# Merging the two halves' token lists of the first sequence before the second sequence's search

## What is computed

```python
r = sigmoid(x @ Wr.T); k = x @ Wk.T; v = x @ Wv.T
scaled = k * v / clip(scale, 1e-10)         # scale = exp(pos * log(sigmoid(decay)))
out = r * cumsum(scaled, axis=1) * scale
normed = (out - mean) * rsqrt(var + eps)    # mean and var over the whole sequence
x = x + (normed * gn_weight + gn_bias) @ Wo.T
```

```python
top_vals, top_idx = top_k(xf @ w_router.T, 4)
g = silu(x_ec @ w_gate[e]); u = x_ec @ w_up[e]
contrib = ((g * u) @ w_down[e]) * w_ec      # added to the tokens' rows
combined = combined + (silu(xf @ w_sh_gate) * (xf @ w_sh_up)) @ w_sh_down
```

## Time and profile before

| | us |
|---|---|
| median of 3 runs | 709.51 |
| lowest and highest | 709.04, 709.54 |
| the profiled execution | 709.04 |
| its span in the trace | 707.2 |
| PE busy | 666.2 (94%) |
| DVE busy | 325.5 (46%) |
| ACT busy | 161.2 (23%) |
| POOL busy | 219.7 (31%) |

### The profile page before, as it was taken

How to read it: one execution, slowest core, us unless ns; L and a number is a source line. 1 busy time by engine, 2 the same in 40 slices (tenths; PEclk the granted TensorE clock), 3 DMA queues, 4 the chain that set the end, 5 groups by cost and what they waited for, 6 DMA issues and landing times. The chain is left out here.

```text
span 707.2 us, 8987 instructions
## 1 busy us (share of the span) xinstructions
PE 666.2 (94%) x3227; PEld 401.1 (57%) x3227; DVE 325.5 (46%) x784; ACT 161.2 (23%) x259; POOL 219.7 (31%) x209
## 2 busy tenths in 40 slices
PE   3999999999999999999999999999999999999881
PEld 2587878878878754455445454554554554544330
DVE  5887567859958771322323323323232333232220
ACT  4833114623211411111112112111111211111110
POOL 4637546535548131021221121212212022212111
PEclk9999999999999999999999999999999999999996
DMA  8201015722775987599999999999999999999972
GB/s 323 71 1 60 1 31 186 263 73 98 289 294 197 355 309 270 212 359 370 405 396 394 371 387 387 404 382 376 388 403 396 359 395 397 391 401 371 388 272 40
DMA packets 52347, 202.67 MB, mean 287 GB/s; under 512 B 7331, under 2 KB 7459, under 8 KB 51920
## 3 DMA queue, kind: packets, MB, share of 16 engines
q1 hardware_dynamic: 36512, 169.23, 60.6%
q0 software_dynamic: 8928, 21.33, 12.7%
q10 hardware_dynamic: 6864, 11.54, 4.4%
HBM read 178.66 MB, written 23.59 MB: 286 GB/s over the span
## 5 line engine op out<-in xcount | busy, mean ns | idle before, releaser
L617 POOL DMA_INDIRECT out_dram<-ym,midx x32 | 51.3, 1603 | 302.8 <-DVE ym L1224 129.4
L1560 PE MATMUL bank<-w_sb,xT 128*64 128x384 f32 x768 | 129.4, 489 | 1.3 <-ACT xT L840 0.8
L1348 PE MATMUL bank<-x_hi,w_parts 128*128 128x512 f32 x368 | 114.9, 395 | 5.0 <-DVE x_lo L953 3.4
L1581 PE MATMUL bank<-w_sb,guT 128*64 128x512 f32 x384 | 88.0, 593 | 3.2 <-issue 2.4
L1560 PEld LDWEIGHTS bank<-w_sb,xT 128*64 128x64 f32 x768 | 52.9, 137 | 64.7 <-issue 59.7
L1348 PEld LDWEIGHTS bank<-x_hi,w_parts 128*128 128x128 f32 x368 | 69.4, 189 | 21.3 <-DVE x_lo L953 4.2
L1348 PE MATMUL bank<-x_lo,w_parts 128*128 128x512 f32 x184 | 71.0, 395 | 0.0
L1164 DVE TENSOR_TENSOR gu<-sg,bank 128x384 f32<-128x384 f32 x32 | 17.7, 554 | 111.4 <-issue 104.5
L1481 PE MATMUL bank<-sh_sb,xS 128*128 128x384 f32 x192 | 63.9, 486 | 0.0
L1581 PEld LDWEIGHTS bank<-w_sb,guT 128*64 128x64 f32 x384 | 27.7, 137 | 52.1 <-issue 51.4
L1481 PEld LDWEIGHTS bank<-sh_sb,xS 128*128 128x128 f32 x192 | 35.7, 191 | 22.3
(11 more groups left out here) (181 smaller groups left out, 949.3 us busy)
## 6 DMA issues: line engine op xcount, KB each, us to landing
w_sb<-in_L_ffn_w_down SPq DMA_DIRECT2D x64, 768.0 KB
w_sb<-in_L_ffn_w_gate SPq DMA_DIRECT2D x48, 768.0 KB
w_sb<-in_L_ffn_w_up SPq DMA_DIRECT2D x48, 768.0 KB
extra<-in_L_ffn_w_gate SPq DMA_DIRECT2D x16, 768.0 KB
extra<-in_L_ffn_w_up SPq DMA_DIRECT2D x16, 768.0 KB
ring<-in_L_attn_x SPq DMA_DIRECT2D x14, 256.0 KB, 3.4
xt_dram<-xwT ACTq DMA_DIRECT2D x12, 256.0 KB, 3.2
xS<-xt_dram SPq DMA_DIRECT2D x12, 256.0 KB, 14.3
```

Source lines behind the costliest of these rows:

```text
L617: pool.indirect_dma_start(out=out[:, :], out_offset=bass.IndirectOffsetOnAxis(ap=midx[j % 3][u][:, :], axis=0), in_=ym[u][:, :], in_offset ...
L1348: ins = pe.matmul(ps[u][:, :], w, xp, start=(n == 0), stop=(n == len(parts) - 1))
L1560: ins = pe.matmul(ps[e * C:(e + 1) * C, 0:I], xT[:, c, e * C:(e + 1) * C], gate_up(2 * j + u, e, k)[:, c, :], start=(c == 0), stop=(c == K ...
L1581: ins = pe.matmul(pair_bank(j, u)[e * C:(e + 1) * C, :], guT[0][:, c, e * C:(e + 1) * C], down(2 * j + u, e)[:, c, :], start=(c == 0), sto ...
```

## The change

In the first search the results go to `best` instead of `key`, and the last round raises `best_ready`. PE gets one more product, `move_best(0)`, between its steps S+5 and S+6: it waits for that semaphore and moves the upper halves' lists into the bank `ps_t[1]`. DVE gets two new functions. `halves_together`, behind S+5, puts the lower halves' lists and the moved ones side by side into `cand`, 64 rows of 128 columns. `merge_rounds` finds the 64 largest of each row in 8 rounds, 4 behind S+5 and 4 behind S+6, and writes them to the last columns of `key` on the first 64 partitions. The other 64 partitions get -1 there. The change of `ramp` moves from behind S+5 to behind S+6. The second search still reads 576 columns, and the move and the maximum in the tail stay.

```diff
+        cand = tile("cand", [E, 2 * C], at=xin_at + 1024)
...
                 keys = key[:, 0:HALF + b * C]
                 for k in rounds:
-                    found = best[:, 8 * k:8 * k + 8] if b else key[:, HALF + 8 * k:HALF + 8 * k + 8]
-                    if b and k == C // 8 - 1:
+                    found = best[:, 8 * k:8 * k + 8]
+                    if k < C // 8 - 1:
+                        seq.then(dve.max(found, keys))
+                        seq.then(dve.match_replace(keys, found, keys, -1.0))
+                    else:
                         dve.max(found, keys).then_inc(best_ready, 1)
-                        dve.wait_ge(best_ready, 1)
-                        break
-                    seq.then(dve.max(found, keys))
-                    if k < C // 8 - 1:
-                        seq.then(dve.match_replace(keys, found, keys, -1.0))
+                        dve.wait_ge(best_ready, b + 1)
...
+            def halves_together():
+
+                seq.then(dve.tensor_copy(cand[:, 0:C], best[0:E, :]))
+                dve.wait_ge(best_moved, 1)
+                seq.then(dve.tensor_copy(cand[:, C:], ps_t[1][0:E, 0:C]))
+
+            def merge_rounds(rounds):
+
+                for k in rounds:
+                    found = key[0:E, HALF + 8 * k:HALF + 8 * k + 8]
+                    seq.then(dve.max(found, cand[:, :]))
+                    if k < C // 8 - 1:
+                        seq.then(dve.match_replace(cand[:, :], found, cand[:, :], -1.0))
...
                 elif s == STEPS + 5:
+                    halves_together()
+                    merge_rounds(range(4))
+                elif s == STEPS + 6:
+                    merge_rounds(range(4, 8))
+                    seq.then(dve.memset(key[E:P, HALF:], -1.0))
+
                     seq.then(dve.tensor_scalar(ramp[:, :], ramp[:, :], -float(T), None, ALU.add))
...
-            dve.wait_ge(best_moved, 1)
+            dve.wait_ge(best_moved, 2)
...
-            def move_best():
-
-                pe.wait_ge(best_ready, 1)
-                pe.matmul(ps_u[0][0:E, 0:C], ident[:, E:P], best[:, :], start=True, stop=True).then_inc(best_moved, 1)
+            def move_best(b):
+
+                pe.wait_ge(best_ready, b + 1)
+                pe.matmul((ps_t[1], ps_u[0])[b][0:E, 0:C], ident[:, E:P], best[:, :], start=True, stop=True).then_inc(best_moved, 1)
...
+                if s == STEPS + 5:
+                    move_best(0)
...
-            move_best()
+            move_best(1)
```

## The result

| | before | changed |
|---|---|---|
| median of 5 runs (us) | 709.54 | 714.86 |
| lowest and highest (us) | 709.04, 711.25 | 713.75, 717.33 |
| ratio, 95% interval | | 1.0081 [1.0056, 1.0106] |
| the profiled execution (us) | 709.04 | 719.23 |

The changed kernel is slower, as forecast, but by 5.3 us instead of 3.1, and 714.86 lies just above the range's end of 714.6. It also spreads more: 3.6 us between its runs against 2.2. Its profiled execution is slower than any of the five timed ones, so what follows first describes a bad case; the experiments' profiles show better ones.

A forecast was written before the change was run, and what follows sets the result against it. The prediction took PE to bound the changed steps and the experts. PE's 3.1 us delay, with merge, clock and slot order at nothing, added to the 709.51 us median gave 712.6 us, range 711.3 to 714.6.

The forecast's parts named there:

- What bounds the kernel: At the changed steps and through the experts PE sets the pace without slack; the DMA delivers in time.
- Where the wait is: PE idles about 2.5 us between S+5 and S+6, ahead of the moved product, until DVE's round 8 ends.
- The gap's size: S+6 on PE starts at 190.5 instead of 187.4 us: a delay of 2.75 to 3.25 us, taken as 3.1.
- the wake and the move: PE's time from round 8's end to S+6: lows 0.05 and 0.2 us, highs 0.24 and 0.40, plus 0.11 restart.
- The clock: PE's products behind the gap before S+6 keep the upper clock; slow products add nothing to the sum.
- the clock falls in the gap: Rival, chance 0.07: eight products behind PE's gap run at the lower clock, adding 1.9 us, 714.5 us in all.
- The merge: DVE's merge rounds, 0.74 us each, stay hidden behind S+5 and S+6, with 2.0 and 0.9 us of cover left.
- The slots' order: New row order in the experts' gathers and scatter-adds: taken as zero, with -0.6 or +0.6 us kept for the range.
- Absorbed at the end: Rival, chance 0.10: the last chain of scatter-adds absorbs PE's 3.1 us delay, leaving 709.5 us, so not slower.

The follow-up runs named there:

- the wait alone: Kernel before plus only the PE move product between S+5 and S+6 that waits for DVE's round 8, result unused, no merge: 715.55 us, ratio 1.0079.
- a lag of 2 us put in: Kernel before with ACT's sigmoid of S+0 repeated three times, delaying the second sequence's vector work: 710.88 us, ratio 1.0011.
- the move inside S+6: Changed kernel with only PE's move placed 24 products later, between v and k of S+6, DVE's order untouched: 711.15 us, ratio 1.0016.
- the variant with the later move: Changed kernel with PE's move behind S+6 instead of S+5 and DVE's merge work placed later too: 710.66 us, ratio 1.0008.
- the changed kernel's second profile: Changed kernel run again without any edit, beside three of the experiments: 716.87 us, ratio 1.0082.

## Why the prediction was wrong, point by point

- **What bounds the kernel: right.** PE's delay at S+6 arrives in full at the experts (9.4 us at both places in the changed kernel's profile), and nothing between absorbs it.
- **Where the wait is: right.** PE's idle note ahead of the move, released by round 8, is there in all profiles of the changed kernel, and the wait alone, without the merge, costs as much as the change.
- **The gap's size: a term of the sum that was mis-sized.** The sum read the end of round 8 as 189.91 from one trace and took it for a property of the kernel. In the execution whose DVE stood where that trace had it, the step was exact to 0.3 us (2.8 us measured, 3.1 forecast, 2.75 to 3.25 as bounds). But in the changed kernel's two profiles round 8 ends at 194.34 and 192.1, and the gaps are 6.38 and 4.25 us. The bounds were those of the wake and the move, a few tenths, while the largest unknown, the time of the other side of the wait, got none. It could hardly be seen in the times of before: there PE does not wait for DVE at this place, and even a lag of 2 us put in costs only 0.8 us.
- **The clock: the step that failed, and a misjudged chance.** The sum put the slow products at nothing, and the rival "the clock falls in the gap" got 0.07. It is what happens in all profiles with the whole gap, at 2.39, 4.25 and 6.38 us alike. The rival's price of 1.9 us is near the smaller of the measured ones (1.7, 2.0, 2.3 and 2.9), in part by luck: it took 8 slow products at 0.24 us more each from the kernel's start, where they stand 0.47 us apart (PEclk reads 1.00 in 15 to 20 us of that trace, so that the lower level was read from the distances alone), while here each costs 0.20 more (0.43 against 0.227) and there are about 8 to 14 of them (1.7 and 2.9 divided by 0.20). The argument against the rival was that the clock read 1.00 in 690 to 694 us with 1.3 us of idling; that told of a gap half as long, not of this one. The measured gap of the wait alone with its slow products gives 709.5 + 2.8 + 1.7 = 714.0 us, so of the 2.2 us between the forecast's 3.1 and the measured 5.3 the clock is the larger part. The rest to 714.86 fits a larger lag in the median execution, of which there is no trace; in the changed kernel's first profile and in that of the wait alone, 0.8 and 0.9 us also came behind the experts' start.
- **The merge: right.** 0.70 us a round where 0.74 was forecast, hidden behind both steps, the second time with 0.53 us left. The cover was the stall itself, as the forecast said; where the stall is gone and the merge stays behind S+5 (the move inside S+6), DVE has no wait for PE left ahead of S+6's and S+7's `kv`. That kernel is 0.16%, 1.1 us, slower than the one before. The move's own 0.5 us on PE are a part of it; that the missing cover is the rest is not shown, as the way from the output projection to the experts' first product is no longer in its profile than before (62.86 us, from 205.56 to 268.42, against 62.92, from 203.73 to 266.65).
- **The slots' order: right to take as nothing.** The variant with the later move has the new order and is at 1.0008 [0.9999, 1.0017].
- **Absorbed at the end: did not happen.** In the changed kernel's profile the add that stood at 623.99 us comes at 633.39, 9.40 us later, as much as the experts' first product.

## What to carry to other kernels

Before a wait is put on the engine that bounds the kernel, ask where the other side stands at that moment and how much that varies between executions: slack hides the variation, and the new wait makes all of it visible. Putting the wait later in the bound engine's row, behind work that doesn't need it, took it off the path here (0.1 to 0.2% over the kernel before was left, against 0.8%), and filling the gap with useless products was cheaper than idling. On PE, count a gap of a few microseconds with the slow products that follow it, in this kernel another 1.7 to 2.9 us.

## What the runs showed of the hardware

- After 25 us of continuous products PE idled for 2.39 us, and its granted clock fell to half right behind the small product that followed (1.00, then 0.59 and 0.56 in the stretches of 2 us). It cost 1.7 us; behind gaps of 4.25 and 6.38 us the slow products cost 2.9 and 2.0 to 2.3 us, so the price did not follow the gap's length. In these longer gaps the clock fell while PE still stood (PEclk 0.90 and 0.96 in 190 to 192 us). With 2.88 us of products first and then 1.56 us of idling the clock stayed at 1.00. The Trainium skill ("TensorE: Matmul & The Clock Gate", Part 1: The HAM clock gate) says that the clock falls after idling and rises after sustained work; the traces agree with both.
- The same DVE product took 0.69 us alone and up to 1.75 us with POOL at work (S+4's in the changed kernel's second profile), and the same chain of DVE work 39.6 to 42.2 us; the longest ones are those in which it overlaps POOL's more.
- A DMA store of 256 KB that ACT waits for let its next step start at 148.84 and at 149.63 us in the two profiles of the changed kernel, and at 147.57 in that of the kernel before, whose instructions up to there are the same. Where this comes from stays open.
